# A two-convolution kernel on one core: the first quad's means move to TensorE, and part of its kernel exponents to GpSimd

## The reference

```
x = x + conv9x9(groupnorm(x), gaussian_kernels(weight0)) + bias
x = x + conv5x5_circular(reflect_pad(groupnorm(x)), weight1)

groupnorm: 16 groups of 2 channels; (g - mean) / sqrt(var + 1e-5)
gaussian_kernels, per pair (output, input channel), from sx, sy, angle:
    q(x, y) = ia*x*x + 2*ib*x*y + id*y*y        x, y in -4..4
    ker = exp(-q/2);  ker / sum(ker)
x: (16, 32, 48, 48) float32;  weight0: (32, 32, 3);  weight1: (32, 32, 5, 5)
```

## Time and profile before

| | |
|---|---|
| runs (three) | 244.45, 244.54, 245.26 us; median 244.54 us |
| profiled execution, first to last instruction (span) | 242.7 us |
| TensorE busy | 232.7 us, 96% of the span |
| VectorE busy | 212.9 us, 88% |
| ScalarE busy | 155.7 us, 64% |
| GpSimd busy | 4.4 us, 2% |
| chain that ended last | PE 71%, DVE 16%, ACT 6%, issue 3%, DMA 2% |

### The profile page before, as it was taken

One profiled execution on the slowest core, in us unless ns is written; L12 is line 12 of the kernel. 1 busy time (PEld: TensorE's weight loads), 2 busy tenths in 40 slices (PEclk: granted clock), 3 DMA queues, 4 the chain that ended last, 5 costly groups with the idle time before them and its releaser, 6 DMA issues.

```text
span 242.7 us, 4170 instructions
## 1 busy us (share of the span) xinstructions
PE 232.7 (96%) x1447; PEld 144.7 (60%) x1447; DVE 212.9 (88%) x463; ACT 155.7 (64%) x333; POOL 4.4 (2%) x12
## 2 busy tenths in 40 slices
PE   5699999899999999999999999999999999999995
PEld 5467666555566665555666665556666665655554
DVE  4989999699999999999989998999997359978943
ACT  5888898999399567999537592537358003569210
POOL 1000000050000000000000000000000000000000
DMA  6980022220015000003412000063020001521123
GB/s 207 379 332 4 6 72 54 69 64 0 3 41 167 7 1 0 0 3 101 136 75 97 0 4 0 12 185 115 1 100 0 0 0 46 163 101 55 48 97 97
DMA packets 8709, 17.24 MB, mean 71 GB/s; under 512 B 3312, under 2 KB 5616, under 8 KB 8688
## 3 DMA queue, kind: packets, MB, share of 16 engines
q1 hardware_dynamic: 7712, 16.64, 20.9%
q10 hardware_dynamic: 976, 0.34, 0.5%
HBM read 5.57 MB, written 4.72 MB: 42 GB/s over the span
## 4 chain that ended last, share of the span: by engine, by line
PE 71%; DVE 16%; ACT 6%; issue 3%; DMA 2%; ACTq 0%; DVEq 0%
PE banks L1425 34%; PE banks L1442 33%; DVE X L766 4%; PE banks L1389 3%; ACT junk L1059 3%; DVE lo L733 2%; DMA tab<-in_tables 2%; DVE whl L563 2%; PE banks L1501 1%; DVE work L558 1%; DVE s L703 1%; DVE partU L719 1%; ACT hi L1115 1%; PE banks L1375 1%; DVE s L706 1%
## 5 line engine op out<-in xcount | busy, mean ns | idle before, releaser
L1425 PE MATMUL banks<-hi,whl 128*128 128x360 f16 (+4 forms) x576 | 99.1, 320 | 1.4 <-ACT hi L1115 1.2
L1425 PEld LDWEIGHTS banks<-hi,whl 128*128 128x128 f16 x576 | 56.0, 99 | 35.7 <-issue 1.7
L1425 PE MATMUL banks<-lo,whl 128*128 128x376 f16 (+4 forms) x288 | 51.6, 320 | 0.5 <-DVE lo L733 0.5
L1059 ACT ACTIVATE junk<-X 128x576 bf16<-128x576 f32 x58 | 39.5, 681 | 2.1 <-DVE X L766 0.5
L1425 PEld LDWEIGHTS banks<-lo,whl 128*128 128x128 f16 x288 | 28.0, 98 | 17.9 <-DVE lo L733 1.1
L1442 PE MATMUL banks<-lo,wh 128*128 128x384 f16 (+1 forms) x165 | 31.8, 323 | 0.0
L1442 PE MATMUL banks<-hi,wh 128*128 128x384 f16 (+1 forms) x165 | 31.8, 323 | 0.0
L1442 PE MATMUL banks<-hi,wl 128*128 128x384 f16 (+1 forms) x165 | 31.8, 323 | 0.0
L1115 ACT CAST hi<-work 128x416 f16<-128x416 f32 x32 | 16.6, 536 | 19.9 <-PE banks L1442 14.1
L1115 ACT CAST hi<-s 128x384 f16<-128x384 f32 x32 | 15.3, 508 | 17.9 <-DVE s L700 12.2
L1105 ACT ACTIVATE work<-work,gof,gsc 128x26 f32<-128x26 f32 (+1 forms) x48 | 23.3, 576 | 3.6 <-DVE gof L644 3.6
(11 more groups left out here) (138 smaller groups left out, 231.7 us busy)
## 6 DMA issues: line engine op xcount, KB each, us to landing
X<-in_x SPq DMA_DIRECT2D x8, 576.0 KB, 9.6
out<-X SPq DMA_DIRECT2D x7, 576.0 KB, 3.0
work<-X SPq DMA_DIRECT2D x8, 432.0 KB, 3.8
whl<-work SPq DMA_DIRECT2D x24, 64.0 KB, 2.0
work<-X SPq DMA_DIRECT2D x8, 144.0 KB, 3.6
stage<-in_w SPq DMA_DIRECT2D x1, 640.0 KB, 7.6
work<-X SPq DMA_DIRECT2D x32, 12.0 KB, 2.3
out<-X SPq DMA_DIRECT2D x1, 384.0 KB, 2.6
```

Of the source, the lines that this page charges most:

```text
L1059: nc.scalar.activation(waste, image(n, m), function, accum_out=sums[c][:, col:col + 1]).then_inc(sums_done[c], 1)
L1425: ins = nc.tensor.matmul(dst[:, :, o0:o1], w[1][:, i, t * P:(t + 1) * P], src[:, :, o0 + dx:o1 + dx], start=(first and part == 0 and t == ...
```

## The change

- TensorE makes all four plain sums of the first quad (`plain`): six matmuls by `group_t` per pair, each over two rows of both images, added up in bank 3; VectorE reduces 96 columns per image there (`first_means`). ScalarE's two plain sums and VectorE's two are left out, and ScalarE keeps the four sums of squares.
- GpSimd makes the far half (taps 3 and 4 off the centre) of `ca`; VectorE makes the near half, and waits for the far one before the arguments of taps 0 and 1. Exp waits for it too, since Exp overwrites `centre`, which GpSimd reads.
- Exp goes in two parts (taps 2 to 4, then 0 and 1), and so do the two block sums. The steps of the statistics stand between them, one or two at a time.
- All ten late warming matmuls and five of the eleven early ones go; `near_rows` starts only behind the statistics.
- On VectorE `scaled(block1(1))` now stands ahead of `first_stream2`.

```
-WARMING = (11, 10)
+NEAR_OFFSETS = 2
+EXP_PARTS = ((2, NT), (0, 2))
+WARMING = 6
+PLAIN_BANK, PLAIN_ROWS = 3, 2
...
-    return 2 * QI * qd - (IMG if c == 1 and qd > 0 else 0)
+    return 2 * QI * qd - (QI if c == 1 and qd > 0 else 0)
...
             def exponents(first, last):
                 btf = bt[:, :, :].rearrange("p e o -> p (e o)")
+                if first == 0:
+                    dve.wait_ge(far_offsets, 1)
...
+            def outer_blocks(part):
+                dve.wait_ge(exp_done, part + 1)
+                at = slice(*EXP_PARTS[part])
+                done(tt(slot(2)[:, at, :], block1(0)[:, at, :], block1(2)[:, at, :], ALU.add))
...
+            def all_blocks(part):
+                dve.wait_ge(dve_w, MARK["outer blocks", part])
+                at = slice(*EXP_PARTS[part])
+                done(tt(slot(1)[:, at, :], slot(2)[:, at, :], block1(1)[:, at, :], ALU.add))
...
+            def first_means():
+                dve.wait_ge(plain_mm, IMG)
+                sums_of = banks[:, PLAIN_BANK, 0:QI * PLAIN_ROWS * W].rearrange("p (i y) -> p i y", i=QI)
+                step(nc.vector.tensor_reduce(first_mean, sums_of, AX_X, ALU.add))
...
-                offsets(1, PAD1)
+                offsets(1, NEAR_OFFSETS)
+                exponents(2, PAD1)
                 exponents(0, 2)
-                first_plain_sums()
-                exponents(2, PAD1)
-                first_stats()
-                block_sums()
+                first_means()
+                outer_blocks(0)
+                first_variance()
+                all_blocks(0)
+                first_guess()
+                outer_blocks(1)
+                first_newton()
+                all_blocks(1)
+                second_root()
+                tap_pairs()
+                first_scales()
                 kernel_sum()
...
+                scaled(block1(1), "block1")
                 first_stream2()
-                scaled(block1(1), "block1")
...
-                act.wait_ge(dve_w, max(MARK["exponents"], MARK["offsets"]))
-                nc.scalar.activation(ker[:, :, :], arg[:, :, :], ACT.Exp).then_inc(exp_done, 1)
+                act.wait_ge(far_offsets, 1)
+                for first, last in EXP_PARTS:
+                    act.wait_ge(dve_w, max(MARK["exponents", first], MARK["offsets"]))
+                    nc.scalar.activation(ker[:, first:last, :], arg[:, first:last, :], ACT.Exp).then_inc(exp_done, 1)
...
+            pool.wait_ge(dve_w, MARK["offset parts"])
+            nc.gpsimd.tensor_tensor(*offset_operands(NEAR_OFFSETS + 1, PAD1), ALU.add).then_inc(far_offsets, 1)
...
+            def plain(n):
+                pe.wait_ge(x_loaded[n], 16)
+                part = PLAIN_ROWS * ROW
+                dst = banks[:, PLAIN_BANK, n * part:(n + 1) * part].rearrange("p (m t x) -> p t m x", m=IMG, x=W)
+                steps = T // PLAIN_ROWS
+                for k in range(steps):
+                    src = pair(n)[:, k * part:(k + 1) * part].rearrange("p (t m x) -> p t m x", m=IMG, x=W)
+                    ins = nc.tensor.matmul(dst, group_t, src, start=(k == 0), stop=(k == steps - 1))
+                ins.then_inc(plain_mm, 1)
...
-            warming(WARMING[0])
+            warming(WARMING)
+            for n in range(2):
+                plain(n)
+            stats(1, 0)
             pe.wait_ge(identity_loaded, 16)
-            for n in range(2):
-                pe.wait_ge(x_loaded[n], 16)
-            near_rows(1, range(2))
-            stats(1, 0)
-            near_rows(1, range(2, 6))
+            near_rows(1, range(6))
             near_rows(2, range(6))
-            warming(WARMING[1])
```

More of the change, by code:

```diff
@@ L252, in build @@
         first_step_done = sem("first_step_done")
+        far_offsets = sem("far_offsets")
         factors_made = sem("factors_made")
@@ L366, in w2_at, with offset_operands @@
             return g2t[:, i, :, :].rearrange("p j (e o) -> p j e o", o=C)
+        def offset_operands(first, last):
+            n = last - first + 1
+            at = slice(first - 1, last)
+            return (ca[:, at, :].rearrange("p k (e o) -> p k e o", o=C), centre.unsqueeze(1).to_broadcast([P, n, NE, C]),
+                    ak[:, at, :].unsqueeze(2).to_broadcast([P, n, NE, C]))
         def flat2(v):
@@ L487, in exponent_parts @@
                         q[:, 7, :].unsqueeze(1).to_broadcast([P, PAD1, C]), mul))
+                MARK["offset parts"] = count[0]
                 done(tt(bt[:, :, :], per_row(yy_t), per_chan(q[:, 10, :]), mul))
@@ L491, in offsets, with tap_pairs @@
             def offsets(first, last):
[L493 to L496, removed]
+                done(tt(*offset_operands(first, last), ALU.add))
                 MARK["offsets"] = count[0]
                 stage_end()
[L500 to L504, removed]
             def exponents(first, last):
                 btf = bt[:, :, :].rearrange("p e o -> p (e o)")
+                if first == 0:
+                    dve.wait_ge(far_offsets, 1)
                 for t in range(first, last):
                     done(stt(arg[:, t, :], btf, float(t - PAD1), ca[:, PAD1 - t - 1, :], ALU.mult, ALU.add))
[L510 to L518, removed]
+                MARK["exponents", first] = count[0]
+            def outer_blocks(part):
+                dve.wait_ge(exp_done, part + 1)
+                at = slice(*EXP_PARTS[part])
+                done(tt(slot(2)[:, at, :], block1(0)[:, at, :], block1(2)[:, at, :], ALU.add))
+                MARK["outer blocks", part] = count[0]
+            def all_blocks(part):
+                dve.wait_ge(dve_w, MARK["outer blocks", part])
+                at = slice(*EXP_PARTS[part])
+                done(tt(slot(1)[:, at, :], slot(2)[:, at, :], block1(1)[:, at, :], ALU.add))
+                MARK["all blocks"] = count[0]
+            def tap_pairs():
+                dve.wait_ge(dve_w, MARK["all blocks"])
+                done(tt(by_two, slot(1)[:, 0:2, :], slot(1)[:, 2:4, :], ALU.add))
             def kernel_sum():
-                done(tt(by_two, slot(1)[:, 0:2, :], slot(1)[:, 2:4, :], ALU.add))
                 stage_end()
@@ L1055, in channel_sums @@
                         act.wait_ge(x_loaded[n], 16)
-                    for kind, function in kinds if (c, n) != (1, 1) else kinds[1:]:
+                    for kind, function in kinds:
                         wait(act, sums_done[c], before + count)
@@ L1370, in stats @@
                 if (c, qd) == (1, 0):
-                    pe.wait_ge(first_plain, IMG)
+                    nc.tensor.matmul(STAT[1][:, QI:], group_t, sums[1][:, QI:], start=True, stop=True).then_inc(stat_mm, 1)
+                    return
                 if shared:
```

67 lines of the change are left out of this document (42 added, 25 removed).

## The result

| | before | after |
|---|---|---|
| median of 18 runs each, taken side by side | 244.49 us (244.40 to 245.26) | 245.06 us (244.80 to 246.95) |
| ratio after / before, 95% interval | | 1.0032 [1.0019, 1.0044] |
| profiled execution, span | 242.7 us | 244.87 us, span 243.1 us |

The medians lie 0.57 us apart (0.23%), and the ratio of the means is 1.0032 with an interval that lies wholly above 1: slower by 0.2 to 0.4%. Forecast were 244.8 us, 0.28 above before, and a difference too small to be told from none; with 18 runs each it can be told. The 18 runs do not lie around one value: nine stand at 244.80 to 244.95, five at 245.16 to 245.43, three at 246.50 to 246.62 with a mean granted clock of 0.993 where the others read 1.0, and one at 246.95. The profile is of the first group. The median falls between the first two groups; without the last four executions it would be 244.9.

The account below looks back on a forecast made before the run. TensorE, 96% busy, gains mainly by an earlier convolution start, set by VectorE and ScalarE. VectorE reaches the statistics at 9.62 + 1.31 = 10.93; the first turned cast follows 12.25 later, so everything moves +0.28: 244.8 us, range 243.3 to 246.0.

Parts of the forecast that it names:

- The near offsets beside GpSimd: VectorE's 768 columns of offsets take 0.96 us instead of 1.76 for 1536, plus a hold by GpSimd's far half.
- D: Time for which GpSimd's far half holds VectorE up: 1.31 us, range 0.9 to 1.9.
- Rival 1: GpSimd's far half costs VectorE nothing; the plain sums then bound the statistics' start, 244.1 us; chance 20%.
- rival 2: GpSimd is slow; VectorE, then Exp and the statistics, wait for `far_offsets`, from D = 1.0 on; 245.4 to 249.3 us; 15%.
- E: Time at which VectorE reaches the statistics: 9.62 plus D, 10.93 us, against 11.76 before.
- The statistics between block sums: On VectorE, `gof` ends at E + 4.45 against 2.68 before; the mix lengthens the statistics by 1.77 us.
- S: Start of stream 1 on ScalarE, at E + 4.45 + 0.10 us; 14.53 before.
- C: First convolution matmul on TensorE, at S + 4.87 us; 20.07 before.
- T: ScalarE's cast of the first turned product, at E + 12.25 us; 22.90 before.
- Rival 4: The rest follows VectorE's stream 1 weights, up to 1.3 us earlier, not ScalarE's casts; 243.3 us; chance 13%.
- The plain sums on TensorE: Sums ready at 10.2 us, following the second pair's landing, so E cannot be earlier; the move costs nothing.
- Rival 3: Clock falls while TensorE idles 2.3 us before the convolution, losing 1.7 us; 246.5 us; chance 7%.

Follow-up runs that it names:

- the statistics run: Changed kernel with all steps of the statistics in one piece ahead of the block sums; 244.16 us, 0.9979 of before.
- the kernel with GpSimd's half: Kernel before, with GpSimd making the far half of the offsets and the near taps' exponents first; 245.23 us, 1.0047 of before.
- the kernel with 3.39 us of idle time: Changed kernel with ScalarE's cast of the stream 1 weights one normalisation later, no warming added; 247.50 us, 1.0117 of before.

## Why the prediction was right, and where it was off

- **The near offsets beside GpSimd: mechanism right, size short.** The step "so I take twice that, 1.21, and 0.1 for the semaphore" gave D = 1.31; measured 1.50, and 0.70 net of the saved 0.80, also in the kernel before. The doubling of a one-input hold was the weak link: the hold was what remained of GpSimd's instruction. The estimate of 1.69 by the Trainium skill, GPSIMD Engine Reference, § 3.1, missed by as much on the other side as a hold, and fits GpSimd's row as counted from the end of VectorE's instruction before (1.68). Rival 1 (GpSimd runs freely) fell with three runs. Of rival 2, the point "from D = 1.0 on" was passed, but not in its way: the net loss came from the hold, not from waiting for `far_offsets`; VectorE's exponents and Exp showed no wait for it.
- **E, when VectorE reaches the statistics:** forecast 10.93, measured 11.13. The 0.19 of D is nearly the whole difference.
- **The statistics between block sums:** forecast from E to the end of `gof` 4.45, measured 4.38. Forecast was that the mix pays 1.77 for weights that come early and that nobody needs. The size holds for the whole stretch (4.38 against 2.67 before), but not for the mix: in one piece the stretch takes 3.14, so 1.24 is the mix and 0.47 the reduction of the plain sums, which comes with their move to TensorE. The run with the statistics in one piece gained 0.90 by undoing the mix.
- **S to C to T:** S 15.48 forecast, 15.61 measured; C 20.35 and 20.47; T 23.18 and 23.31. The chain through ScalarE holds to 0.01 from S on. Rival 4 (the rest follows VectorE's weights), which would have shown marks that move by other amounts than the end, fell: all moved by about 0.40.
- **The profiled execution:** 244.8 forecast, 244.87 measured. The marks moved by 0.40 instead of 0.28; that the two times lie nearer to each other is owed to the median of before, which was 244.54 in the three runs that the prediction had and 244.49 beside the change.
- **The plain sums on TensorE were the second term that was sized wrongly, and the median shows it.** The step "The sums are there at 8.04 + 1.95 + 0.2 = 10.2" let them follow the landing of the second pair and made their end a constant. In the profile they ended at 10.48 and waited for no load: the 24 records run through, and their end hangs on when the clock rises. It varies from execution to execution: 4.58 or 5.79 for the 24, as the spacing changed near 6.9 or near 9.5 us. "So this move costs nothing" holds for the profiled execution alone. Before, VectorE and ScalarE made these sums, and TensorE had only two `near_rows` products ahead of the statistics. Kernels with the change's plain sums and its start of TensorE spread by 0.6 to 1.3 in executions at full clock (the one at 246.95 aside), that of before by 0.3 in three batches of four (244.41 to 244.71, 244.34 to 244.60, 244.44 to 244.77; in the fourth one execution stands at 245.26). The late warming of the kernel before can hide a delay of up to 0.5 on ScalarE's way to the convolution, which would narrow its spread too; but in the kernel with GpSimd's half, where VectorE's delay goes through TensorE, the seven executions at full clock spread by only 0.18. An estimate for the changed kernel: with the plain sums at 11.62, as in the statistics run, the reduction comes 0.5 later than at 11.13, and the time is 245.4, at the upper end of its five at 245.16 to 245.43. No late execution of the changed kernel itself was caught in a profile, so that these five are of this sort is argued and not shown; the start of VectorE's chain, which varied by 0.29 over the profiles, has a part in the smaller differences.
- **Where luck comes in.** That the median lies 0.26 above the forecast and not farther is in part chance: it fell between the nine executions of the forecast's path and nine later ones, whose causes the prediction had as a constant (the plain sums) or as a rival of 7% (the clock).
- **Rival 3 (the clock falls)** came in 3 of 18 executions, at its price: 246.5 forecast, 246.50 to 246.62 measured. That an idle time can do this was shown with 3.39 us before the convolution and, in the kernel with GpSimd's half, with 2.19 us before the statistics (five of 12 executions, one of them profiled; 1.69 between the medians of the two groups); that the 2.0 us of the changed kernel did it in these three was not seen in a profile, and the one at 246.95 with a clock of 1.0 stays unexplained.

## What to carry to other kernels

An addition given to GpSimd was not free here for VectorE, as both read two operands from SBUF: count what remains of GpSimd's instruction as a wait on VectorE, and move the work only where VectorE does something else meanwhile. Put long independent work between short dependent steps only if no one waits for the last of these; here ScalarE did, and the other result was early for nobody. Work moved to TensorE near the start of a program runs at whichever level the clock has by then, and that differed from one execution to the next, so look at the spread of the runs as well as at one profile. An earlier start of TensorE, on a constant that needs no load, went with the narrowest spread and the best time here.

## What the runs showed that was not expected

- The hold is the remainder of GpSimd's row, less 0.14, at 384 and at 768 columns (0.68 and 1.50).
- The clock's rise at the start varies by over 2 us between executions of programs that start TensorE at about the same time (near 6.9, 7.4, 8.3 and 9.5 us in four profiles), and the granted clock in the rows reads 1.00 all the while. A start 1.5 us earlier did not bring it forward in the one profile of it (7.1).
- The late rise reaches the end by two ways: through the reduction on VectorE, and through the `near_rows` products that stream 1 reads.
- The fall of the clock differs from execution to execution at the same idle time: in the kernel before (1.50 us) 6 of 35, 3 of 23, 0 of 23 and 0 of 18 executions in the four batches; in the kernel with GpSimd's half alone (2.19 us) 5 of 12; in the kernel with 3.39 us of idle time 4 of 6, two of them with about twice the loss.
